# Gated cross-attention block with a ternary-weight FFN on one core: pairs of tiles from the first on, small steps, floors and scores regrouped, w3's product four tiles behind

## The reference

```python
def _bitlinear(x, w):            # rmsnorm, rows to 8 bits, weights to -1, 0, 1, product
    xn = _rmsnorm(x)
    return einsum('bsd,hd->bsh', act_quant(xn), weight_quant(w))
...
a = 0.6 * sigmoid(si[:, :, None] + sj[:, None, :] + b[0]) + 0.4 * layernorm(x)   # si, sj = ctx @ Wi, ctx @ Wj
x = x + tanh(g_xattn[0]) * a
h = silu(_bitlinear(layernorm(x), w1)) * _bitlinear(layernorm(x), w2)
x = x + tanh(g_ffn[0]) * _bitlinear(h, w3)
```

## Time and profile before

| | |
|---|---|
| median of 3 runs | 170.49 us (170.19 to 172.68) |
| the profiled execution: its own time | 171.08 us |
| its span, first to last instruction | 169.3 us |
| mean granted clock of PE over the span | 0.948 of 2.4 GHz |
| PE, DVE, ACT, POOL busy | 146.1, 127.5, 108.9, 118.3 us |
| read from and written to HBM | 13.89 MB and 4.19 MB |

### The profile page before, as it was taken

How to read it: one execution, slowest core, us unless ns; L and a number is a source line. 1 busy time by engine, 2 the same in 40 slices (tenths; PEclk the granted TensorE clock), 3 DMA queues, 4 the chain that set the end, 5 groups by cost and what they waited for, 6 DMA issues and landing times.

```text
span 169.3 us, 2504 instructions
## 1 busy us (share of the span) xinstructions
PE 146.1 (86%) x743; PEld 76.9 (45%) x743; DVE 127.5 (75%) x202; ACT 108.9 (64%) x180; POOL 118.3 (70%) x195
## 2 busy tenths in 40 slices
PE   0853963799765999999999999999999999999992
PEld 0712642557335355444444444454544444444440
DVE  0355999996399868999899899599728787587541
ACT  3087889995668827968988957387364535743430
POOL 3113997999998898999788796887973373528700
PEclk9999998558997599999999999999999999999999
DMA  5999999993417416461374245814546425541633
GB/s 131 320 393 369 387 385 414 370 389 133 87 32 143 85 31 127 74 147 31 97 147 85 84 92 136 207 33 85 129 83 147 76 75 107 125 85 44 169 124 124
DMA packets 44149, 26.67 MB, mean 158 GB/s; under 512 B 34663, under 2 KB 36712, under 8 KB 44136
## 3 DMA queue, kind: packets, MB, share of 16 engines
q1 hardware_dynamic: 44128, 26.52, 56.7%
q10 hardware_dynamic: 8, 0.00, 0.0%
HBM read 13.89 MB, written 4.19 MB: 107 GB/s over the span
## 4 chain that ended last, share of the span: by engine, by line
PE 68%; POOL 17%; DMA 6%; issue 4%; SPq 3%; DVE 1%; POOLq 0%; DVEq 0%
PE ps L1215 42%; PE ps L1249 22%; DMA hq<-in_ctx_dram 6%; POOL raw_room L473 3%; POOL raw L473 3%; POOL hqT L476 3%; POOL c_all L427 2%; SPq L276 2%; POOL xq L458 1%; POOL ln_r L412 1%; PE ps L1165 1%; PE ps L1164 1%; SPq L272 1%; PE ps L1154 1%; POOL rnorm L437 1%
## 5 line engine op out<-in xcount | busy, mean ns | idle before, releaser
L1215 PE MATMUL ps<-w1T,xqT 128*128 128x512 f16 (+1 forms) x192 | 42.5, 373 | 1.2 <-ACT raw_room L689 1.2
L1215 PE MATMUL ps<-w2T,xqT 128*128 128x512 f16 (+1 forms) x192 | 42.0, 370 | 0.0
L1249 PE MATMUL ps<-w3T,hqT 128*128 128x512 f16 x176 | 40.1, 379 | 0.0
L980 DVE SCALAR_TENSOR_TENSOR raw<-ps,deq,raw_room 128x1408 f32<-128x1408 f32 x16 | 26.9, 1683 | 15.8 <-PE ps L1215 15.6
L698 ACT ACTIVATE junk<-raw 128x1408 f16<-128x1408 f32 x16 | 22.0, 1375 | 23.1 <-DVE raw L980 23.1
L485 POOL TENSOR_SCALAR hq<-raw,h_scale 128x1408 f16<-128x1408 f32 x15 | 25.8, 1720 | 10.2 <-DVE h_scale L990 10.1
L1215 PEld LDWEIGHTS ps<-w1T,xqT 128*128 128x128 f16 x192 | 19.2, 101 | 23.0 <-issue 2.1
L1215 PEld LDWEIGHTS ps<-w2T,xqT 128*128 128x128 f16 x192 | 19.2, 100 | 21.7 <-issue 3.1
L689 ACT ACTIVATE raw_room<-ps,deq 128x1408 f32<-128x1408 f32 x16 | 22.8, 1426 | 6.9 <-PE ps L1215 6.9
L985 DVE TENSOR_REDUCE h_max<-raw 128x1 f32<-128x1408 f32 x16 | 25.8, 1614 | 0.3
L1249 PEld LDWEIGHTS ps<-w3T,hqT 128*128 128x128 f16 x176 | 17.2, 98 | 19.2
(11 more groups left out here) (97 smaller groups left out, 201.9 us busy)
## 6 DMA issues: line engine op xcount, KB each, us to landing
c_all<-in_x_dram SPq DMA_DIRECT2D x16, 256.0 KB, 9.7
out_dram<-out_ring SPq DMA_DIRECT2D x16, 256.0 KB, 2.0
raw<-in_L_ffn_w_dram SPq DMA_DIRECT2D x4, 704.0 KB, 11.7
raw_room<-in_L_ffn_w_dram SPq DMA_DIRECT2D x3, 768.0 KB, 7.9
raw<-in_L_ffn_w_dram SPq DMA_DIRECT2D x3, 768.0 KB, 11.0
hq<-in_ctx_dram SPq DMA_DIRECT2D x4, 256.0 KB, 9.9
raw_room<-in_L_ffn_w_dram SPq DMA_DIRECT2D x1, 512.0 KB, 10.2
raw<-in_L_ffn_w_dram SPq DMA_DIRECT2D x1, 512.0 KB, 11.4
```

What stands on the lines that cost most here:

```text
L980: v.scalar_tensor_tensor(out=hid[:, t % HS, :], in0=ps_up[:, 0:H], scalar=deq[:, 1, t:t + 1], in1=gate[:, t % GATES, :], op0=ALU.mult, op1 ...
L1215: last = m.matmul(bank[:, lo:hi], xqT[:, i % XT, k, :], wT[w][:, k, lo:hi], start=(k == 0), stop=(k == KD - 1))
L1249: last = m.matmul(ps_y[t % 2], hqT[:, t % HT, k, :], w3T[:, :, k, :], start=(k == 0), stop=(k == KH - 1))
```

## The change

It rewrites the lists of all five queues, and these parts:

- UNITS are eight pairs. `slopes_x` works on groups (SGROUPS) of 2, 2, 4, 4 and 4 tiles, `mean_x` and `th_neg_x` on groups of four (MGROUPS). `intercept` reads the tanh sums itself and no longer waits for `th_neg_x`.
- Floors: `c_all` and the h ring get extra columns that hold the floor and the epsilon. The maxima and the squares are taken over D + 1, D + 2, H + 1 and H + 2 columns, so the floor instructions on DVE and the multiply-add in `step_x` and `dequant_h` on POOL are gone. Two POOL memsets (`hidden_floors`) wait until all of w2 is turned.
- `scale_w` is three instructions instead of five before it releases the conversions; the rest is `weight_factor`, placed later. From unit 1 on one `dequant_x` stands for `dequant_gate` and `dequant_up`.
- Scores: the four small matmuls have two columns (si and sj); `half_scores` scales both; a new PE step `spread_scores` spreads sj by four transposes of a column broadcast. The 512-column float32 matmul is gone. DVE no longer copies ctx; ACT does all four.
- w3's 16-bit form has a buffer of its own (`w3q`) instead of lying in the ring of transposed h.
- The affines of tiles 8 to 15 are on ACT, those of 0 to 7 on POOL, none on DVE. Absolute sums of w2 move in part from ACT to DVE; w1 and w2 conversions are 3 and 2 groups on DVE (2 and 1 before), w3's are 2 (1 before).
- `last_product` starts behind `up_product(2)` and is then about four tiles behind.

```diff
-    UNITS = [(0, 1), (1, 2), (2, 4), ..., (14, 16)]
+    UNITS = [(0, 2), (2, 4), (4, 6), (6, 8), (8, 10), (10, 12), (12, 14), (14, 16)]
+    SGROUPS = [(0, 2), (2, 4), (4, 8), (8, 12), (12, 16)]
+    MGROUPS = [(0, 4), (4, 8), (8, 12), (12, 16)]
-    AFFINE_ACT = [6]
-    AFFINE_DVE = [1, 4, 7]
+    AFFINE_ACT = [4, 5, 6, 7]
+    AFFINE_DVE = []
-    CONV_DVE = [[2, 4], [0], [0]]
+    CONV_DVE = [[0, 3, 5], [2, 3], [0, 3]]
-    OUT_DVE = [[2, 4], []]
+    OUT_DVE = [[3, 5], [2]]
...
-        w3q = hqT[:, :, :, :].rearrange("p s k t -> p s (k t)")
+        w3q = sb("w3q", [P, KD, H], F16)
...
+            def spread_scores(n):
+                pe.wait_ge(scores_sb, n + 1)
+                for k in range(TB):
+                    last = m.transpose(ps_y[1][:, k * P:(k + 1) * P], s_half[:, n * TB + k, 1:2].broadcast_to([P, P]),
+                                       ident32[:, :])
+                last.then_inc(sj_ps, 1)
```

More of the change, by code:

```diff
@@ L537, in _ @@
-            conv_w(2, 3)
-            affine_x(5)
-            quant_x(2)
-            step_x(2)
-            quant_x(3)
-            dequant_up(2)
-            dequant_gate(2)
-            slopes_x(4)
-            slopes_x(5)
-            quant_h(0)
-            mean_x(4)
-            quant_x(4)
-            step_x(3)
+            conv_w(0, 1)
+            affine_x(0)
+            affine_x(1)
+            conv_w(0, 2)
+            conv_w(0, 4)
+            slopes_x(1)
+            quant_x(0)
+            quant_x(1)
@@ new lines, in _ @@
+            affine_x(2)
+            affine_x(3)
+            conv_w(1, 0)
+            conv_w(1, 1)
+            step_x(0)
+            mean_x(0)
+            dequant_gate(0)
+            conv_w(1, 4)
+            conv_w(1, 5)
+            conv_w(2, 1)
+            dequant_up(0)
+            conv_w(2, 2)
+            hidden_floors()
+            quant_x(2)
+            step_x(1)
+            slopes_x(2)
+            dequant_x(1)
+            quant_x(3)
+            affine_x(4)
+            affine_x(5)
@@ L590, in _ @@
-            quant_x(13)
-            dequant_up(7)
-            dequant_gate(7)
-            affine_x(14)
-            affine_x(15)
+            dequant_h(2)
+            quant_x(10)
+            quant_x(11)
+            add_x(4)
+            quant_h(6)
+            step_x(5)
+            dequant_x(5)
             quant_h(7)
             dequant_h(3)
-            step_x(8)
+            quant_h(8)
+            quant_x(12)
+            mean_x(3)
+            quant_x(13)
+            step_x(6)
+            add_x(6)
@@ L750, in _ @@
[L750 to L770 removed]
+            score(1)
@@ L1027, in _ @@
             sum_w(0, 2)
-            stats_x(1)
-            intercept(0)
-            ctx_out(1)
-            scale_w(0)
-            conv_w(0, 2)
-            make_x(0)
-            conv_w(0, 4)
-            half_scores(1)
+            stats_x(0)
+            scale_w(0)
+            conv_w(0, 0)
+            weight_factor(0)
+            conv_w(0, 3)
+            intercept(0)
+            sum_w(1, 0)
+            half_scores(1)
+            sum_w(1, 1)
+            make_x(0)
+            stats_x(1)
@@ L1036, in _ @@
+            max_x(0)
+            conv_w(0, 5)
+            evac_w(0, 3)
             intercept(1)
-            max_x(0)
-            affine_x(1)
+            evac_w(0, 5)
+            sum_w(2, 0)
+            scale_w(1)
             make_x(1)
-            max_x(1)
-            evac_w(0, 2)
-            stats_x(2)
-            scale_w(1)
-            conv_w(1, 0)
-            sum_w(2, 0)
-            evac_w(0, 4)
-            sum_w(2, 1)
+            sum_w(2, 1)
+            conv_w(1, 2)
+            conv_w(1, 3)
@@ L1048, in _ @@
+            stats_x(2)
+            scale_w(2)
+            weight_factor(1)
+            conv_w(2, 0)
+            weight_factor(2)
+            half_scores(2)
+            evac_w(1, 2)
+            clip_w3(0)
+            max_x(1)
             stats_x(3)
+            clip_w3(1)
+            conv_w(2, 3)
+            clip_w3(2)
             intercept(2)
-            stats_x(4)
-            scale_w(2)
-            stats_x(5)
-            conv_w(2, 0)
-            ctx_out(2)
-            clip_w3(0)
+            clip_w3(3)
@@ L1056, in _ @@
+            hidden(0)
+            half_scores(3)
+            max_h(0)
             intercept(3)
             make_x(2)
-            half_scores(2)
-            clip_w3(1)
+            hidden(1)
             max_x(2)
-            clip_w3(2)
+            max_h(1)
             make_x(3)
-            hidden(0)
-            clip_w3(3)
-            max_h(0)
-            half_scores(3)
+            hidden(2)
             max_x(3)
-            hidden(1)
+            max_h(2)
+            stats_x(4)
+            hidden(3)
@@ L1265, in _ @@
             scores(0, "spread", 1)
+            spread_scores(0)
+            sum_w(0, "scores", 1)
             turn_ctx(1)
-            sum_w(0, "scores", 1)
             scores(1, "sums", 1)
```

642 lines of the change are left out of this document (300 added, 342 removed).

## The result

The changed kernel takes 162.01 us (median of 4 runs, 161.96 to 162.48) against 170.79 us for the kernel before beside it: a ratio of 0.9478, 95% interval 0.9439 to 0.9516. It is 8.8 us faster. 164.8 was forecast; the time lies at the fast end of the stated range of 161.5 to 169.5, and outside the forecast's own 163 to 166.8.

The account below looks back on a forecast made before the run. PE's dense product stream behind 63 us was taken as the bound, so only its start counts: 171.08 - 6.3 (earlier start) + 0.6 (holes) = 165.4 as profiled, 164.8 as median; range 161.5 to 169.5.

Parts of the forecast that it names:

- rival three: All lists run at their short durations, no hole: stream starts at 55.0, 162.3 us; chance 0.13.
- The path of w2: w2's scale at 32.3, 3.3 us late, paid back by POOL's fewer conversion groups, through at 38.9: nothing gained or lost.
- DVE behind the scale: DVE's list from 32.3 to tile 2's maximum and reciprocal: tile 2 quantized at 44.0 or 46.1, against 51.06.
- PE from there to gate 1: PE from scale_w(2)'s first instruction, 39.1 or 41.2, to gate 1 at 42.8 or 44.9: nothing gained.
- Then nothing is waited for: On PE behind up 0: no wait for tile 2, which is long turned by then.
- From up 0 to gate 3: PE's work between up 0 and the stream's start: 6.6 us at full clock, 7.9 partly at the slow one.
- The stream's holes: PE idle in the dense stream when later tiles come late: 0.6 us charged, 0 to 3.
- Floors and small steps: Removed floors lighten DVE's and POOL's lists, ACT gets more affines; priced at nothing while the stream covers them.
- Rival one: DVE collides with POOL all through the front: stream starts at 61.3, 169.2 us; chance 0.17.
- Rival two: PE stays at 1.2 GHz from 36 to 50 us, gate 1 and up 0 longer: +2.8, 167.6 us; chance 0.10.
- Rival four: Pairs late for gate 8, 10, 12 and 14, make_x standing behind hidden on DVE: at worst 174.0 us; chance 0.10.
- The signs: Expected in the trace: tile 2 quantized at 44 to 46, up 0 at 46 to 48, stream's start 55 to 58.5.

Follow-up runs that it names:

- the large dose: Changed kernel with max_x(1) on DVE moved behind stats_x(3), two clips and a w3 conversion, just ahead of intercept(2): 167.09 us.
- second trace: The changed kernel itself run again, unedited, as reference on the chip of the last four experiments: 162.39 us, ratio 0.9398.
- the last variant: Changed kernel with DVE's max_x(1) ahead of clip_w3(0) and POOL's quant_x(2) ahead of conv_w(2, 2) and hidden_floors: 163.38 us.

## Why the prediction was right, point by point

The mechanism was right and its direction too. The size was not: the forecast was 164.8 and 162.0 was measured, outside its own range of 163 to 166.8 and inside the wide one by rival three alone. The 2.8 us are a start at 54.4 for the 56.9 that was taken (2.5) and holes of 0.15 for 0.6.

- **What bounds it.** Right: the stream is 103 us before and after, and the gain is 8.6 us of its start.
- **The path of w2.** Right in kind, 0.5 us too late: sum_w(2, 0) began at 29.71 and not at 30.05, and w2's scale was there at 31.8, not 32.3. POOL was through with w2 at 40.6, later than my 38.9: two conversions took 3.72 where I had 2.76, with DVE's make_x beside them, and the power in step_x took 1.43. PE just didn't feel it: its last turn of w2 stood at 40.80, behind the spreading transposes.
- **DVE behind the scale.** make_x(1) took 1.26, not 1.7, and the two conversions 2.52 together, inside my 1.7 to 3.8, so scale_w(2)'s first instruction was over at 38.4 against 39.1 to 41.2. This is 0.7 us better than my best case.
- **PE from there to gate 1. The term that was mis-sized most.** Gate 1 came at 41.0 against 42.8 to 44.9, 1.8 us better than my best case. Of these 1.1 are the stretch from the scale to gate 1 on PE, 2.6 us where I had put 3.7 without a price for each part: scores, 1.02, turns of w2, 0.61 and 0.38, and the spreading, 0.65, followed one another almost without a wait. clip_w3(0) took 1.69, and tile 2 was quantized at 44.05, the early end of my 44.0 to 46.1.
- **"Then nothing is waited for."** Wrong by 1.24 us: since gate 1 came early, tile 2 was late for it. Up 0 ended at 47.85, 0.5 ahead of my best.
- **From up 0 to gate 3.** 6.6 us at full clock, as summed. The spreading transposes cost what turn_ctx's do, 0.60 to 0.65.
- **The stream's holes.** 0.15 us instead of 0.6. Gate 8, up 8 and last 6 didn't wait.
- **Floors and small steps.** Right that they are free in the stream, wrong to price them at nothing ahead of it: put back, they delay its start by 1.0 to 1.2 us (1.6 to 2.0 by the medians, on another chip).
- **Rivals.** Rival three, short durations and no hole, with 162.3, is the one that came; I gave it 0.13. Rival one did happen to single instructions (3.72, 1.69), but not to the list as a whole. Rival two, gate 1 at the slow clock, was not in this trace but in those of two of its variants. Rival four didn't come.
- **The signs.** Up 0 by 48 us, no idle behind it, the holes, the clock from gate 1 on and tile 2 at 44 came as listed; the start at 54.4 is ahead of the 55 to 58.5.

What stays open is how the gain divides. Undone one by one from the changed kernel (tile 2's place by the large dose), tile 2's place is worth 3.8 to 4.0 us by the start of the stream (4.7 to 5.1 by the medians), the small steps 1.0 to 1.2 (1.6 to 2.0), the scores 0.0 to 0.3 (0.6 to 0.9): 4.8 to 5.5 us of the 8.6 together, or 6.9 to 8.0 by the medians. That dose is one that I chose, not the order of the kernel before. And the order alone, put into the kernel before in three steps, gave nothing, so the worth of a part hangs on the others. What w3's lag is worth with the other lists fitted to it wasn't tried, nor were the single first tiles, the places of the affines or w3q's own buffer by themselves.

## What to carry to other kernels

When a stream on one engine is dense and the same length in both kernels, the time is its start plus a constant: look for the first product that waits, and behind it for the next one. A list written by hand is one schedule over all engines; a product moved by one place, or one tile served first, can cost as much as the whole change brings (6 to 12 us here), because what waits for it stands ahead of something else on its own engine. Saved small steps are worth their time only on the way to the first product of the stream, and there these were worth about their sum. And before a start that moved is put down to an edit, look at where the first work behind the loads stands: between two traces it moved by up to 1.8 us here with nothing in the edit to cause it.

## What the runs showed of the hardware

Gate 1 ran at 2.4 GHz (2.54 us) in the changed kernel and at 1.2 GHz in two of its variants (4.23 and 3.96 us). The mean granted clock of 40 to 57 us was 1.00 in the one and 0.90 in the others. What PE did just ahead of gate 1 doesn't tell them apart: the idle times there are 0.65 and 0.20 us in the changed kernel, 0.66 and 0.21 in the variant of 4.23, whose edits touch nothing that PE waits for up to there. Nor is the clock the same for one kernel: from 32 to 34 us the changed kernel's first trace has a granted clock of 0.50 and its second trace 1.00, and over its executions the mean clock goes from 0.978 to 1.00. The Trainium skill, page TensorE: Matmul & The Clock Gate, section "Part 1: The HAM clock gate", says that the number of slow matmuls varies between runs of one kernel; these traces agree.

So a gain of 1 to 2 us ahead of a stream is uncertain: the wait that was removed in the last variant and the slow gate 1 that came with it are of the same size. But the clock doesn't sort the executions by time: the one of 0.978 is the fastest of the changed kernel's six on the later chip (161.28 us), and the same holds for the last variant (161.46).
